# The last two steps of a small product, moved from VectorE to ScalarE and GpSimd

## The reference

```
h = relu(layernorm(x))
# first SAGE layer, W_l1, b1, W_r1
agg  = segment_sum(h[src], dst) / max(degree, 1)
h1   = relu(agg @ W_l1 + b1 + h @ W_r1)
# second SAGE layer
x    = x + (segment_sum(h1[src], dst) / max(degree, 1)) @ W_l2 + b2 + h1 @ W_r2
```

## Time and profile before

| what | value |
|---|---|
| three timed runs | 1647.69, 1649.49, 1650.51 us |
| the profiled execution, whole | 1648.47 us |
| its span (first to last instruction) | 1645.9 us |
| TensorE clock granted, share of full | 0.997 |
| build, about 42 to 477 us | 435 us of the span |
| busy in 62 to 270 us of the build: TensorE, VectorE, ScalarE, GpSimd | 195, 177, 159, 127 of 208 us |

### The profile page before, as it was taken

The page is one execution under the profiler, slowest core; times in us unless marked ns, Lnnn a source line. Parts: engine busy times, 40 slices in busy tenths (PEclk is TensorE's granted clock), DMA queues, the critical chain, the costliest instruction groups (busy, mean ns, idle before and its releaser), DMA issues.

```text
span 1645.9 us, 42637 instructions
## 1 busy us (share of the span) xinstructions
PE 1571.8 (95%) x11401; PEld 1231.4 (75%) x11402; DVE 967.3 (59%) x2866; ACT 620.7 (38%) x1693; POOL 327.5 (20%) x927
## 2 busy tenths in 40 slices
PE   7899998999999999999999999999999999998996
PEld 7555555555567777778888888888888888886885
DVE  6888897888861222243335666666646777777111
ACT  6777787777741111111112222222224444441000
POOL 1565565665530000000000000000002222220000
PEclk9999999999999999999999999999999999999998
DMA  4366585766698776533345666666632222131344
GB/s 138 91 183 161 154 208 145 186 177 161 170 243 229 224 206 188 173 115 124 119 156 148 165 165 165 165 166 168 172 110 71 76 83 83 62 137 65 120 142 154
DMA packets 353545, 245.62 MB, mean 149 GB/s; under 512 B 195242, under 2 KB 337382, under 8 KB 353510
## 3 DMA queue, kind: packets, MB, share of 16 engines
q1 hardware_dynamic: 353510, 245.19, 52.3%
HBM read 138.17 MB, written 99.31 MB: 144 GB/s over the span
## 4 chain that ended last, share of the span: by engine, by line
issue 60%; PE 32%; DVE 3%; POOL 3%; DVEq 1%; SPq 0%; POOLq 0%; DMA 0%; ACT 0%
PE ps L1429 22%; PE ps L1522 8%; POOL work L675 3%; PE ps L1471 1%; DVE e_buf L1021 1%; PE ps L1464 0%; DVE work L967 0%; DVE e_buf L1017 0%; SPq L424 0%; PE ps L1708 0%; DVE e_buf L1037 0%; DVEq L396 0%; DVEq L1017 0%; DVEq L1021 0%; PE ps L1402 0%
## 5 line engine op out<-in xcount | busy, mean ns | idle before, releaser
L1522 PE MATMUL ps<-arena 128*128 128x256 f16 (+1 forms) x5000 | 602.4, 272 | 6.6 <-DVEq L320 1.6
L1522 PEld LDWEIGHTS ps<-arena 128*128 128x128 f16 x5000 | 484.7, 97 | 101.3 <-issue 32.6
L1429 PE MATMUL ps<-e_buf 128*128 128x400 bf16 (+1 forms) x2476 | 381.2, 307 | 30.1 <-DVE e_buf L1021 20.3
L1429 PEld LDWEIGHTS ps<-e_buf 128*128 128x128 bf16 x2476 | 213.0, 97 | 190.7 <-DVE e_buf L1021 64.7
L1516 PE MATMUL ps<-arena 128*128 128x256 f32 x1250 | 278.7, 380 | 2.4 <-DMA arena<-wgt_blocks 2.4
L1516 PEld LDWEIGHTS ps<-arena 128*128 128x128 f32 x1250 | 235.8, 190 | 33.7 <-issue 1.7
L675 POOL TENSOR_TENSOR work<-work 128x256 f32<-128x256 f32 x75 | 59.8, 797 | 957.9 <-ACT work L860 957.9
L1021 DVE TENSOR_SCALAR e_buf<-iota,off_g,front 128x400 bf16<-128x400 f16 (+1 forms) x619 | 231.0, 416 | 32.6 <-PE ps L1429 20.5
L660 POOL TENSOR_SCALAR e_buf<-e_buf,w_col 128x128 bf16<-128x128 bf16 x600 | 216.6, 375 | 165.8 <-DVE e_buf L1017 165.4
L701 ACT ACTIVATE e_buf<-e_buf,front 128x128 bf16<-128x128 bf16 x219 | 88.0, 402 | 108.4 <-DVE e_buf L1017 108.2
L1017 DVE TENSOR_SCALAR e_buf<-iota,front 128x128 bf16<-128x128 f16 x419 | 102.0, 251 | 35.5 <-PE ps L1429 23.4
(11 more groups left out here) (215 smaller groups left out, 1585.7 us busy)
## 6 DMA issues: line engine op xcount, KB each, us to landing
arena<-turned_blocks SPq DMA_DIRECT2D x75, 800.0 KB, 4.3
wgt_blocks<-arena SPq DMA_DIRECT2D x25, 1600.0 KB, 10.3
arena<-wgt_blocks SPq DMA_DIRECT2D x25, 1600.0 KB, 8.7
cnt_blocks<-work SPq DMA_DIRECT2D x25, 800.0 KB, 5.5
turned_blocks<-arena SPq DMA_DIRECT2D x25, 800.0 KB, 3.8
e_raw<-edge_features_padded SPq DMA_DIRECT2D x25, 576.0 KB, 3.9
edge_features_padded<-in_edge_attr SPq DMA_DIRECT2D x24, 512.0 KB, 9.9
out<-arena SPq DMA_DIRECT2D x24, 128.0 KB
```

The lines of the kernel that those rows point to most:

```text
L1429: return pe.matmul(bank[:, 0:wide], rows_, cols, start=start, stop=True, skip_group_check=True)
L1522: m = pe.matmul(into[:, 0:wide], counts[:, b * P:(b + 1) * P], ZH[zin(i)][:, b * ZW + part * D:b * ZW + part * D + wide], start=(b == 0 an ...
```

## The change

ScalarE copies the product out of its PSUM bank into `R_` and raises `s_own`, behind pair 3 of the next chunk. GpSimd waits for that and adds the bias in on-chip memory, behind pair 5, raising a new semaphore, `s_ownB`. VectorE does neither, and its loop has no special first turn any more; GpSimd's has one now. The wait for the early weights (`s_w`) ahead of the loop goes from VectorE to GpSimd. After the build VectorE waits for `s_ownB` where it waited for `s_own`; TensorE's two waits for `s_own` stay.

```
+            def own_bias(n):                       # GpSimd
+                wait(pool, s_own, n + 1)
+                pool.sem_inc(s_made, 1)
+                pool.tensor_tensor(node(R_, n), node(R_, n), b_early[:, 0, :], ALU.add).then_inc(s_ownB, 1)
+
+            def turn(c):
                 packed = pairs_of(pool, mybir.EngineType.Pool, c, "fixed")
                 for i in range(PER):
                     weigh_pair(c, i, packed[i])
                     if i == 6:
                         second(c)
+                    elif i == 5 and not isinstance(c, int):
+                        own_bias(c - 1)
+            pool.wait_ge(s_w, 16 * 16)
+            turn(0)
+            with nc.Fori(1, NT, engines=[pool.engine], hint_back_edge=True) as c:
+                turn(c)
+            own_bias(NT - 1)
...
+            def own_take(n):                       # ScalarE
+                wait(act, s_ownM, n + 1)
+                act.activation(node(R_, n), own_ps, ACT.Copy).then_inc(s_own, 1)
...
+                    elif i == 3 and not isinstance(c, int):
+                        own_take(c - 1)
...
+            own_take(NT - 1)
...
-            def own_take(n):                       # VectorE
-                wait(dve, s_ownM, n + 1)
-                dve.tensor_tensor(node(R_, n), own_ps, b_early[:, 0, :], ALU.add).then_inc(s_own, 1)
-
-            def turn(c):
+            with long_loop(dve, NT) as c:
                 packed = pairs_of(dve, mybir.EngineType.DVE, c, "both")
                 for i in range(PER):
                     hot_pair(c, i, packed[i], packed[PER + i])
-                    if i == 3 and not isinstance(c, int):
-                        own_take(c - 1)
-            dve.wait_ge(s_w, 16 * 16)
-            turn(0)
...
-            own_take(NT - 1)
...
-            dve.wait_ge(s_own, NT)
+            dve.wait_ge(s_ownB, NT)
```

More of the change, by code:

```diff
@@ L238, in build @@
         s_own = sem("own_part_taken")
+        s_ownB = sem("own_part_with_bias")
         s_mo = sem("mean_ready")
@@ L662, in weigh_pair @@
                 m.then_inc(s_hotP, 1)
-            with long_loop(pool, NT) as c:
+            def own_bias(n):
[3 more added lines that the diff above has]
+            def turn(c):
                 packed = pairs_of(pool, mybir.EngineType.Pool, c, "fixed")
@@ L1051, in turn @@
                     hot_pair(c, i, packed[i], packed[PER + i])
-                    if i == 3 and not isinstance(c, int):
-                        own_take(c - 1)
-            dve.wait_ge(s_w, 16 * 16)
-            turn(0)
-            with nc.Fori(1, NT, engines=[dve.engine], hint_back_edge=True) as c:
-                turn(c)
-            own_take(NT - 1)
             chain = drained(dve)
```

## The result

The changed kernel takes 1652.25 us in the median of 13 runs (1649.16 to 1655.98), the kernel before 1648.20 in 13 runs on the same chips. The ratio is 1.0024, with a 95% interval of 1.0016 to 1.0033: slower, by about 4 us. The profiled execution took 1651.17 us.

What follows compares the result with a forecast made beforehand. TensorE and VectorE were taken as close to full, VectorE being the feeder TensorE waits for, by little. 24 chunks x 0.10 = +2.4, halved to +1.2: 1648.47 + 1.2 + 1.02 = 1650.7 us, range 1644.5 to 1656.5.

Steps and rivals of the forecast that it cites:

- outside 42 to 478 us: Times outside the build; a change there was named as a sign that the prediction was wrong.
- VectorE, 0.33 us a chunk removed: Build, VectorE's L1046 removed: gain of 0.33 us a chunk, at most 7.9 us; the other reading was 0.02.
- ScalarE, the copy at nothing: Build, behind L692 of pair 3: the 0.38 us bank copy fills a 0.32 us hole and costs nothing.
- GpSimd, the slot of 0.68: Build, behind pair 5: the new bias addition holds GpSimd for 0.68 us, with bounds 0.62 and 0.98.
- lateness of 0.43: Build, pair 6: GpSimd's L660 comes 0.43 us later; 0.10 a chunk remains if VectorE is 0.33 ahead.
- rival B: Build, pairs 6 and 7: GpSimd's list becomes the bound, 0.41 a chunk, 9.8 us more, 1659.3; chance 0.16.
- How GpSimd pushes VectorE, about 0.4: Build, ahead of pair 6: GpSimd's two-input bias holds VectorE's operation back by about 0.4 us.
- That VectorE was 0.33 ahead by then is spent there: Build, ahead of pair 6: the hold-back of about 0.4 us uses up VectorE's gain of 0.33.
- +2.4 halved to +1.2: Build sum: 24 chunks x 0.10 = +2.4 us, halved because longer chunks, half of them, swallow the lateness.
- Rival A: Build: VectorE stays 0.33 ahead and GpSimd's lateness hides in buffers, 7.9 us less, 1641.6; chance 0.17.
- Rival C: Build: the lock alone counts, VectorE loses 0.42 and gains 0.33 a chunk, +2.2 us, 1651.7; chance 0.10.
- The end of the build: After the last chunk: VectorE's scale work can start up to 2.2 us earlier, but nothing is gained.

Runs made afterwards that it cites:

- e2: e1 with GpSimd's bias left out altogether, so ScalarE copies and nobody adds the bias; 1648.49 us, 0.9993 of the kernel before.
- e1: The changed kernel with the special first turn of VectorE's build loop given back; 1650.68 us, 0.9997 of the kernel before.
- e7: e1 with VectorE instead of ScalarE copying the bank, behind pair 3, while GpSimd adds the bias; 1650.68 us, 1.0003 of the kernel before.
- e5: The changed kernel with 40 useless semaphore increments on VectorE behind the build; 1656.15 us, 1.0035 of the kernel before.
- e11: The changed kernel with 28 useless semaphore increments on VectorE behind the build; 1648.37 us, 0.9981 of the kernel before.
- e6: The changed kernel run once more, with no edit; 1653.79 us, 1.0018 of the kernel before.
- e4: e1 with ScalarE's copy moved behind pair 0 and GpSimd's bias behind pair 2; 1648.73 us, 0.9990 of the kernel before.
- e9: e1 with three useless semaphore increments on VectorE after the build; 1647.02 us, 0.9975 of the kernel before.
- e3: e2 with VectorE adding the bias in layer one, behind its mean of each tile; 1645.27 us, 0.9968 of the kernel before.
- e10: e3 run once more, unaltered; 1645.77 us, 0.9964 of the kernel before.
- e8: e3 with 40 useless semaphore increments on VectorE; 1649.93 us, 0.9998 of the kernel before.
- e12: The kernel before with 100 useless semaphore increments in VectorE's layer one, 50 at tile 1 and 50 at tile 24; 1658.80 us, 1.0049.

## Why the prediction was right, and where it was wrong

The forecast was 1650.7 and no change within 0.2%; measured are 1652.25, and a ratio of 1.0024 whose interval spans 0.2% (1.0016 to 1.0033). The size is close by luck, and the reason isn't right: the forecast put +1.2 us into the build and nothing outside it. The build gained, and the loss lies where the prediction said that it would be wrong if a change showed: outside 42 to 478 us.

**VectorE, 0.33 us a chunk removed.** Right in sign, mis-sized: 0.20 (e2 against before, 4.8 us over 24 chunks instead of 7.9). It lies between the two readings of the earlier trace rows, 0.33 and 0.02, and a little closer to the one that I took.

**ScalarE, the copy at nothing.** Right as far as the runs can tell. L738 takes 0.38 to 0.41 us, and in e2, where it is all that was added, the build is only faster.

**GpSimd, the slot of 0.68.** Right: 243.66 to 244.34, the operation 0.73. Its lateness of 0.43 was wrong as a cost. The fetch came at 244.34 and the weighting 0.78 behind it, released by VectorE, where the prediction had 0.52 and VectorE in front. The 0.52 was right as the least distance (0.51 in the trace before), though its own row names VectorE as the releaser. VectorE, held back by the bias itself, came later than GpSimd, and rival B fell with it.

**How GpSimd pushes VectorE, about 0.4.** The mechanism is in the rows, 778 against 434 ns, but on a 400-wide operation. The mark that I named, a 200-wide L1021 of 0.7 ahead of pair 6, did not come (321 ns). The failed step is the next one, "That VectorE was 0.33 ahead by then is spent there". Of the 0.34 to 0.43 held back only 0.09 a chunk reaches TensorE in the mean (2.2 us, e1 against e2) or 0.07 (e7). I had charged it in full in every plain chunk and let the longer ones swallow it. The table of e2 shows another picture: it is there in full in four plain chunks and not at all in the nine others. The sum of the build was so -4.8 + 2.2 = -2.6 in e1, and -1.3 and -2.4 in the two executions of the change (-1.0 and -2.3 in e5 and e11, whose build is the same), instead of +2.4 halved to +1.2. "The plain chunk stays at 15.85 to 15.95" was wrong: 15.67. Rival A had this sign at three times the size. Rival C, the lock alone, had the price right of one block and also charged it in every chunk.

**The end of the build.** Right: nothing.

**What the prediction didn't have at all.** The diff takes away VectorE's special first turn. The kernel before had a first turn written out with constants; the list of VectorE goes from 1180 to 1024 instructions. I described that and gave it no cost. It cost 0.7 us in chunk 0 (e1 gives it back), and it moved every later instruction of VectorE to another place in the list, which put a hole of 2.7 to 3.1 us on the path at tile 24. Before, the hole stood in idle time. Of the forecast's terms none touches layer one. That the time fell into the stated range all the same is luck.

**The ledger.** Chunk 0 +0.7, the rest of the build -1.3 to -2.4, the hole +2.7 to +3.0 and up to 3.4 more where the clock halves behind it. With the hole off the path the change measures 0.9981 and with it 1.0018 to 1.0024: about 0.4%, 6 to 7 us by the ratios. In e6's trace the two parts make 3.0 + 3.4 = 6.4, but that is one execution. The timed runs, each of which has a span and a mean granted clock, split the difference so:

| | changed kernel, 25 runs | e11, 11 runs | difference |
|---|---|---|---|
| mean span | 1651.2 | 1646.6 | 4.6 us |
| mean span of the runs at a clock of 0.996 | 1649.0 (6 runs) | 1646.3 (7) | 2.7 us |
| mean clock | 0.9942 | 0.9955 | 0.0012 |

At the same clock the difference is 2.7 us, the length of the hole. The 0.0012 of clock are 4.0 us more at 1.2 GHz, which cost 2.0 us. So the 3.4 us that e6 lost to the clock are not the rule. What is left up to 6 to 7 can lie between the chips, on which the kernel before has medians from 1648.20 to 1650.85.

**What the holes are.** The traces know two queues that carry instructions, q8 and q14. Between 477 and 700 us q14 carries five packets in each of the 14 traces. In the kernel after, first the whole stretch and then the hole alone (queue, packets, MB, share of 16 engines):

```profile
q14 instruction: 5, 0.04, 0.1%
```

```profile
q14 instruction: 1, 0.01, 1.3%
```

It is so in every trace. Times are in us, a hole from the end of one neighbour in VectorE's list to the start of the next:

| trace | hole | q14 packets that start in it | TensorE's wait for VectorE there | clock at 1.2 GHz |
|---|---|---|---|---|
| before | 501.98 to 504.55 | 502.24 | - | - |
| after | 688.26 to 691.01 | 689.23 | 2.4 | - |
| e6 | 687.88 to 690.97 | 689.19 | 2.8 | 6.8 from 691.0 |
| e5 | 492.46 to 498.04 | 496.21 | 3.9 | 3.4 from 499.7 |
| e11 | 499.66 to 502.21 | 500.30, 501.99 | - | - |
| e1 | 507.38 to 510.28 | 508.19 | 2.3 | 3.4 from 511.7 |
| e4 | 507.34 to 510.30 | 508.52 | 2.4 | - |
| e2 | 504.90 to 507.78 | 505.67 | 2.3 | 3.4 from 509.1 |
| e9 | 498.96 to 501.17 | 499.44, 499.63 | - | - |
| e7 | 503.75 to 505.75 | 504.02 | - | - |
| e3 | 497.45 to 499.86 | 498.07, 498.54 | - | - |
| e10 | 497.64 to 499.82 | 498.02, 498.65 | - | - |
| e8 | 480.63 to 484.57 | 482.60 | 3.5 | 6.8 from 485.0 |
| e12 | 487.48 to 492.49 | 490.69 | 8.2 | 10.2 from 489.6 |

With five packets in 223 us, chance would put one into few of the 14 holes. So a hole is tied to an instruction transfer, and that VectorE waits in it for its own instructions is by far the likeliest reading. It is still not shown by an experiment: no run took the transfer away, no row says for which engine a packet is, and other packets of q14 come without a hole.

## What to carry to other kernels

Ask of every diff what it does to the length and layout of each engine's instruction list, a special first turn above all: that alone moved this kernel by 0.4%, more than the edit itself (0.2%). Look for a gap that nothing releases, and for an instruction packet in it. When a small change gives a small result, measure it also with a few useless instructions in front of the next stage; if three of them change the verdict, it was never a verdict on the edit. A delay of an operation on VectorE is not worth a fixed fraction of itself at TensorE. Here it was worth all of it in four plain chunks of 13 and nothing in the others, 0.09 us a chunk in the mean over all. So read several chunks before pricing it, and put the full price in every chunk at the end of the range and not in the sum.

## What the runs showed of the hardware

- **Holes in VectorE's list.** Gaps of 2.0 to 5.6 us with no releaser stand near the start or the end of layer one, one in each of the 14 traces, and an instruction packet starts in each of them (table above). Their place repeats between executions of one kernel (L1187 to L1188 in both of the changed kernel, L1087 to L1099 in e3 and e10), between kernels with the same list there (e1, e2 and e4; before, e7 and e9), and shifts with 3, 28, 40 or 100 instructions added. A gap of 2.2 us near 885 us between two register instructions is none: VectorE runs one operation of 2.55 us meanwhile.
- **The clock can fall around such a wait of TensorE.** Of the eight traces in which TensorE waited 2.3 us or more behind a hole, six have it at 1.2 GHz for 3.4 to 10.2 us, beginning in the wait or within 1.2 us of its end; the first execution of the changed kernel (2.4 us) and e4 (2.4 us) have none, so it doesn't always come. e6 shows 0.51 of full for 6 us. In e1 5 us behind the hole that ended at 510.49 have a mean of 0.66, so 3.4 us of them at 1.2 GHz:

```profile
511.00:516.00 5.00, 4.66 (x23) 3.62 (x24) 1.26 (x4) 0.38 (x1) 0.00 (x0) 0.66 0.99 329
```

  Where an expectation above gives the time of a fall, it is that of the clock's records, some 11 us later than the time in the rows.
- **A two-input operation of GpSimd holds back the operation that VectorE starts behind it,** not one that already runs: in the changed kernel the bias starts at 243.66, the 400-wide operation that VectorE began at 243.30 ends at 243.81, and the next, begun at 243.73, takes 778 ns instead of 434. A 128-wide one takes 673 instead of 245 beside L650. The Trainium skill, "SBUF — State Buffer", section "Who interferes with whom", has this as an exclusive lock on a shared port pair, which blocks a VectorE operation in a two-port mode if it comes second. The trace agrees on who waits for whom; no row shows the mode. In the mean three quarters of the delay didn't reach TensorE (0.09 of about 0.35 us).
- **A semaphore increment on VectorE takes 0.093 us** from one to the next (e11).
